# Nine bias columns instead of 37 are turned into rows, GpSimd fills its constants earlier, and the first stages stand in another order

## The reference, cut to what matters

```python
nx = layer_norm(x) ;  q = nx @ Wq ;  k = ctx @ Wk ;  v = ctx @ Wv
evidence = softmax(q k^T / sqrt(128)) @ v
combined = [nx, evidence, anchor]                      # anchor: one vector per batch
router_probs = softmax(combined @ router_W + router_b)             # 3 experts
h = silu(combined @ e_w1 + e_b1) ;  expert_out = h @ e_w2 + e_b2   # 3 x 256 hidden
g = sigmoid(silu(combined @ gate_w1 + gate_b1) @ gate_w2 + gate_b2)
x = x + g * (sum(expert_out * router_probs) @ out_w + out_b)
xq, xkv = ada_ln(x, cond), ada_ln(ctx, cond)           # silu(cond) @ Wss + bss
x = x + softmax over 16 heads of 8 (xq @ Wq + bq, xkv @ Wkv + bkv) @ Wp + bp
```

## Time and profile before

| what | value |
|---|---|
| median of 3 runs | 202.46 us (201.9 to 203.8) |
| the profiled execution | 201.29 us, its span 199.5 us |
| busy: PE, DVE, ACT, POOL | 188.9, 159.5, 126.8, 54.7 us |
| chain that ended last | PE 75%, DVE 14%, ACT 6%, issue 3% |
| HBM read, written | 11.29 MB, 2.88 MB |

### The profile page before, as it was taken

The page is one execution under the profiler, slowest core; times in us unless marked ns, Lnnn a source line. Parts: engine busy times, 40 slices in busy tenths (PEclk is TensorE's granted clock), DMA queues, the critical chain, the costliest instruction groups (busy, mean ns, idle before and its releaser), DMA issues.

```text
span 199.5 us, 4395 instructions
## 1 busy us (share of the span) xinstructions
PE 188.9 (95%) x1503; PEld 132.2 (66%) x1503; DVE 159.5 (80%) x478; ACT 126.8 (64%) x280; POOL 54.7 (27%) x75
## 2 busy tenths in 40 slices
PE   1999999999999999998999999999999999999992
PEld 0679878877767885785566856866658554566551
DVE  7747937787769999999999998999698979984021
ACT  0442458656870389578754596199929765989950
POOL 2758579949239410002470000001000200000000
PEclk9996999999999999999999999999999999999997
DMA  4991010125477000054036200032242430000001
GB/s 122 304 357 63 8 20 22 28 79 108 110 200 202 7 1 0 18 130 111 12 97 153 70 30 0 6 87 62 74 138 71 110 71 1 1 2 3 5 0 52
DMA packets 12199, 14.65 MB, mean 73 GB/s; under 512 B 1896, under 2 KB 9938, under 8 KB 11602
## 3 DMA queue, kind: packets, MB, share of 16 engines
q1 hardware_dynamic: 12120, 14.37, 26.4%
q10 hardware_dynamic: 58, 0.01, 0.0%
HBM read 11.29 MB, written 2.88 MB: 71 GB/s over the span
## 4 chain that ended last, share of the span: by engine, by line
PE 75%; DVE 14%; ACT 6%; issue 3%; POOL 0%; ACTq 0%; DVEq 0%; POOLq 0%
PE ps L735 67%; PE ps L738 8%; DVE mx L1318 5%; ACT tz L663 2%; ACT tz L672 2%; DVE hT L1241 2%; DVE xn L1177 1%; DVE bias_rows L1060 1%; DVE p L1208 1%; ACT probs L700 1%; DVE qr L1313 1%; POOL rstd L521 0%; DVE qp L1311 0%; DVE nm L1199 0%; ACT p L612 0%
## 5 line engine op out<-in xcount | busy, mean ns | idle before, releaser
L1318 DVE TENSOR_REDUCE mx<-ps 128x1 f32<-128x512 f32 x128 | 82.3, 680 | 4.1 <-PE ps L735 4.0
L700 ACT ACTIVATE probs<-ps 128x512 f32<-128x512 f32 x128 | 65.5, 603 | 6.3 <-PE ps L735 6.2
L735 PE MATMUL ps<-k_st,q_st 125*128 125x512 bf16 x128 | 38.8, 380 | 0.6 <-issue 0.6
L735 PE MATMUL ps<-q_st,k_st 128*128 128x256 bf16 x256 | 35.9, 273 | 0.2 <-DVE mx L1318 0.2
L735 PE MATMUL ps<-probs,vtile 128*32 128x256 f32 x512 | 30.9, 382 | 0.1
L735 PEld LDWEIGHTS ps<-q_st,k_st 128*128 128x128 bf16 x256 | 23.1, 98 | 11.1 <-issue 1.7
L735 PEld LDWEIGHTS ps<-probs,vtile 128*32 128x32 f32 x512 | 15.2, 109 | 12.5 <-ACT probs L700 1.8
L735 PEld LDWEIGHTS ps<-k_st,q_st 125*128 125x128 bf16 x128 | 11.8, 98 | 12.3 <-ACT probs L700 2.9
L663 ACT ACTIVATE tz<-ps,half_b 128x256 f32<-128x256 f32 x28 | 12.0, 474 | 10.0 <-PE ps L735 9.9
L1241 DVE SCALAR_TENSOR_TENSOR hT<-ps,biases,tz 128x256 f32<-128x256 f32 x28 | 12.2, 478 | 4.4 <-ACT tz L672 4.4
L529 POOL TENSOR_TENSOR rstd<-ve,mhalf 128x2 f32<-128x2 f32 x4 | 3.0, 760 | 45.0 <-DVE ve L1284 45.0
(11 more groups left out here) (173 smaller groups left out, 308.8 us busy)
## 6 DMA issues: line engine op xcount, KB each, us to landing
k_st<-k_scr SPq DMA_DIRECT2D x24, 192.0 KB
q_st<-q_scr SPq DMA_DIRECT2D x16, 144.0 KB
k_scr<-kp SPq DMA_DIRECT2D x12, 128.0 KB, 2.4
w<-in_L_xcond_e_w SPq DMA_DIRECT2D x3, 384.0 KB, 4.4
c_sb<-in_ctx SPq DMA_DIRECT2D x4, 256.0 KB, 4.5
q_scr<-qp SPq DMA_DIRECT2D x12, 64.0 KB, 2.0
x_sb<-in_x SPq DMA_DIRECT2D x4, 128.0 KB, 4.4
out<-y_sb SPq DMA_DIRECT2D x4, 128.0 KB, 2.2
```

Of the source, the lines that this page charges most:

```text
L700: A.activation(probs[:, g % 2, j, half * 2 * T:(half + 1) * 2 * T], bank("unit", b, u), ACT.Exp)\
L735: return nc.tensor.matmul(out, lhsT, rhs, start=start, stop=stop)
L1318: V.tensor_reduce(mx[:, b, t, h:h + 1], bank("tile", b, i), AX_X, ALU.max, negate=True)\
```

## The change

Four things are changed.

- The bias columns are laid out as 28 that are read as columns (seven for each batch), then the nine that are read as rows. Only the nine are split, turned (27 rows instead of 111) and sent; `bias_rows` has nine blocks instead of 37, so its memset writes 576 words in each partition instead of 2368.
- On POOL `vt0` (the constants) stands ahead of `rsx.0`; `identb` stands behind four fills of `k_st`.
- The lists are in another order: on PE `nxT.0` and `P4` stand ahead of `P2` and `P5`, `P6` stands between the two halves of `s0.0`; on ACT `nxTe.0` is the first, then `p4a`, then `ctxTe.0`. The banks of 213 of the 443 PE tokens are others. Behind batch 0 the moves are mostly of a few places.
- On SP the three stores of the first batch's keys stand in the order 2, 1, 0.

```diff
-NBZ = NZ + 1
-C_EB = B * NBZ
+C_LG = B * NZ
+C_EB = C_LG + B
 C_GB = C_EB + E
 C_BO = C_GB + 1
 NCB = C_BO + 1
+NRB = NCB - C_LG
...
     "pool": """
-        ident rsx.0 vt0 identb rsc.0 cn.0 rsx.1 zer.0 zer.1 zer.2 zer.3 zer.4 gw2h zer.5 rsx.2 rsc.2 kp.0.0 cn.2
...
+        ident vt0 rsx.0 rsc.0 cn.0 zer.0 zer.1 zer.2 zer.3 identb rsx.1 gw2h zer.4 zer.5 zer.6 zer.7 rsx.2 rsc.2
...
     "sp": """
-        ones brows k_out.0.0 k_out.0.1 k_out.0.2 k_in.0.0 k_in.0.1 k_in.0.2 k_in.0.3 q_out.0.0 k_out.1.0 q_out.0.1
...
+        ones brows k_out.0.2 k_out.0.1 k_out.0.0 k_in.0.0 k_in.0.1 k_in.0.2 k_in.0.3 q_out.0.0 k_out.1.0 q_out.0.1
...
-        half_b = sb("half_b", [P, C_EB])
+        half_b = sb("half_b", [P, C_LG])
         wide_b = sb("wide_b", [P, P])
-        bias_r = sb("bias_r", [P, 2, NCB])
-        bias_p = sb("bias_p", [P, NP, NCB], BF16)
-        bias_t = sb("bias_t", [NP * NCB, P], BF16)
-        bias_rows = sb("bias_rows", [P, NCB, P], BF16)
+        bias_r = sb("bias_r", [P, 2, NRB])
+        bias_p = sb("bias_p", [P, NP, NRB], BF16)
+        bias_t = sb("bias_t", [NP * NRB, P], BF16)
+        bias_rows = sb("bias_rows", [P, NRB, P], BF16)
...
-                mm(ot, onesb[:, 0:P], bias_rows[:, b * NBZ + NZ, 0:E], stop=False)
+                mm(ot, onesb[:, 0:P], bias_rows[:, b, 0:E], stop=False)
...
-                V.tensor_copy(bias_p[:, 0, :], biases[:]).then_inc(s["prep_dve"], 1)
+                V.tensor_copy(bias_p[:, 0, :], biases[:, C_LG:]).then_inc(s["prep_dve"], 1)
```

More of the change, by code:

```diff
@@ L48 @@
     "pe": """
[L49 to L78, removed]
@@ new lines @@
+        P1@4 ctxT.0@7 P3@6 nxT.0@4 P4@0 P2@1 P5@2 qm.0@6 P5g@4 s0.0.1@3 P6@2 s0.0.0@6 P6b P5b@7 P6c ctxT.1@6
+        p0T.0.1@1 p0T.0.0@5 P8@6 P5c@3 pc.0.0@4 nxT.1@7 pc.0.1 hkvT.0@1 qm.1@5 hid.0.0@0 hid.0.6@4 hid.0.1 P7@7
+        kproj.0@1 hid.0.2@7 hid.0.3 s0.1.1@5 hid.0.4@1 hid.0.5 lgT.0.0@2 lgT.0.1 P8b@4 vproj.0@7 s0.1.0@2 hkvT.2@3
+        eo.0.2@4 p0T.1.1@0 eo.0.3 eo.0.0@7 nxT.2@5 eo.0.1 p0T.1.0@3 ctxT.2@2 hkvT.1@1 qm.2@6 nxT.3@5 pc.1.0@3 pc.1.1
+        kproj.1@6 s0.2.0@4 lgT.1.0@7 xqT.0@5 s0.2.1@0 lgT.1.1 qproj.0@5 hid.1.2@4 hid.1.3 hid.1.4@5 hid.1.5
@@ new lines @@
+        p0T.2.1@0 hid.1.0@3 hid.1.1 vproj.1@0 kproj.2@4 qm.3@2 p0T.2.0@6 hid.1.6@5 ctxT.3@1 pc.2.0@6 tile.0.0@7
+        tile.0.1@2 tile.0.2@1 pc.2.1 tile.0.3@3 tile.0.4@5 tile.0.5@0 tile.0.6@7 tile.0.7@6 eo.1.2@4 tile.0.8@5
+        tile.0.9@7 eo.1.3 eo.1.0@3 tile.0.10@0 tile.0.11@5 tile.0.12@6 eo.1.1 tile.0.13@2 hid.2.0@1 rows.0.0@7
+        hid.2.1 tile.0.14@2 tile.0.15@0 hid.2.6@6 hid.2.2@7 hid.2.3 lgT.2.0@3 lgT.2.1 unit.0.0@5 unit.0.1@4
+        unit.0.2@1 unit.0.3@2 unit.0.4@3 hid.2.4@0 unit.0.5@7 tile.0.16@4 unit.0.6@2 hid.2.5 tile.0.17@1 s0.3.0@4
@@ new lines @@
+        tile.1.2@4 kproj.3@2 tile.1.3@7 tile.1.4@1 rows.0.3@4 tile.1.5@3 p0T.3.1@5 xqT.2@0 tile.1.6@6 tile.1.7@4
+        tile.1.8@2 tile.1.9@3 qproj.2@0 tile.1.10@7 tile.1.11@5 tile.1.12@4 pv.0.4@6 pv.0.5 unit.0.24@0 unit.0.25@3
+        pc.3.0@4 unit.0.26@6 unit.0.27@5 unit.0.28@3 pc.3.1 unit.0.29@6 tile.1.13@7 tile.1.14@1 unit.0.30@3
+        unit.0.31@5 tile.1.15@2 tile.1.16@0 tile.1.17@4 lgT.3.0@7 tile.1.18@5 tile.1.19@1 tile.1.20@6 tile.1.21@3
+        lgT.3.1 rows.1.0@0 hid.3.2@1 tile.1.22@0 hid.3.0@3 tile.1.23@6 hid.3.1 hid.3.4@2 unit.1.0@6 unit.1.1@0
@@ new lines @@
+        unit.1.2@4 unit.1.3@7 hid.3.5 tile.1.24@3 unit.1.4@7 tile.1.25@6 unit.1.5@4 unit.1.6@5 unit.1.7@0
+        tile.1.26@3 hid.3.3 tile.1.27@7 tile.1.28@0 tile.1.29@3 tile.1.30@5 tile.1.31@4 tile.2.0@6 pv.0.6@0 pv.0.7
+        tile.2.1@3 vproj.2@7 rows.1.1@0 hid.3.6@2 tile.2.2@4 oT.0.0@1 tile.2.3@7 rows.1.2@3 tile.2.4@5 oT.0.1@0
+        tile.2.5@4 tile.2.6@3 eo.3.2@2 eo.3.3 eo.3.0@5 rows.1.3@4 eo.3.1 unit.1.8@0 unit.1.9@6 unit.1.10@1
+        unit.1.11@7 unit.1.12@4 unit.1.13@2 unit.1.14@0 unit.1.15@3 tile.2.7@1 tile.2.8@5 tile.2.9@7 pv.1.0@0 pv.1.1
@@ L828, in widen_biases @@
                 pe.wait_ge(s_brows, 16)
[L829 removed]
+                mm(o[:, 0:P], onesb[:, 0:P], bias_rows[:, C_BO - C_LG, :]).then_inc(s["prep"], 1)
             def output_weights(name, part, k0, k1):
```

170 lines of the change are left out of this document (90 added, 80 removed).

## The result

The changed kernel takes **205.53 us** (204.07 to 206.31, 6 runs), the kernel before 202.38 us (201.03 to 206.1, 6 runs): a ratio of 1.0161, 95% interval [1.0118, 1.0203]. It is slower by 1.6%, some 3.2 us, and outside the forecast range of 200.3 to 204.9. The profiled execution is the slowest of the six, 206.31 us with a span of 204.5. Beside the one profiled before (201.29 us, span 199.5) it overstates the loss, so sizes in time are taken from the ratios and the mechanisms from the rows.

The account below looks back on a forecast made before the run. TensorE was taken as the bound, its start held by DMAs. P4's wait +0.7 and reordered later stages -0.1 made +0.6 us on the median 202.46: 203.1 us, range 200.3 to 204.9.

Parts of the forecast that it names:

- The bound and the early x: At the start, xn.0 ends 1.4 us earlier but gains nothing, since P5 waits for its weights until about 7.5.
- the rival: At the start, the x path was the bound: up to 1.4 us faster; no chance given.
- a fixed wall at 7.5: Ahead of P5 on TensorE, the DMA of its weights lands at about 7.5, so P5 can't start before.
- P4 ahead of P5: On TensorE before the scores, P4 waits for ACT's last small DMA until 8.5; scores start at 11.7, +0.7 us.
- With the rise at the same moment: From P5 to the scores, TensorE's pace rises at 9.6 as before, so P5 ends at 10.4 and P5g at 11.7.
- rival 3: TensorE's pace after the idle 1.6 us rises later, near 13 us: +2.4, 204.8 us; chance 0.18.
- The table load: ACT's 1.28 us load moves between nxT.0 and nxTe.0, hidden behind P5: no cost; the skill's 1380 ns drain doesn't show.
- Interleaved P6: Between 16.5 and 20 us, breaking up small products may remove the half-clock stretch: 0 or -1.7 us, taken as 0.
- rival 1: The slow stretch at 16.5 goes, since small products no longer stand together: -1.7, 201.4 us; chance 0.22.
- Smaller edits: Splits, P7, p2, fills and key stores move on no path, cost nothing; reordered later stages give -0.1 us.
- The only case in my list on this side: The slower rival, TensorE's pace rising near 13 us: 204.8 us; chance 0.18.

Follow-up runs that it names:

- The two kernels with nine columns: Changed code with the kernel before's order lists: 202.25 us, 1.0002; the same with GpSimd's constants ahead of rsx.0: 201.87 us, 0.9995.
- the two best kernels: Changed kernel with P4 back behind P5g, plus waits between three GpSimd fills (200.74 us, 0.9913) or two fills moved each way (201.83 us, 0.9952).
- the best version: Changed kernel with P4 back behind P5g and GpSimd waits ahead of fills 5, 6 and 7: 200.74 us, ratio 0.9913 to the kernel before.
- the four changed kernels without the long hold: Changed kernel with fills moved (1.0025) or gaps between fills (0.9992), and each of these with P4 behind P5g (0.9952, 0.9913).
- the first group: Changed kernel with P4 behind P5g (1.0040), fills moved (1.0025), both (0.9952); and the kernel before with P4 early (1.0022).

## Why the prediction was wrong

**The bound and the early x.** Right, within the noise. The two kernels with nine columns, 0.54 us of memset and in the second 0.60 us of cast, are at 1.0002 and 0.9995, with intervals that shut out the 1.4 us of the rival. The DMA of P5's weights is seen as P5's releaser in the two best kernels, where `nxT.0` starts at 6.34 and 6.24 and P5 at 7.70 and 7.72. It isn't a fixed wall at 7.5: with the nine columns alone P5 starts at 7.37, and with the constants moved too its releaser is `m_qk`, at 7.98.

**P4 ahead of P5.** The mechanism is right, and its first numbers too: 2.08 us of idle TensorE, P4 at 8.87, P5 at 9.69, against 1.6, 8.5 and 9.3. The size at the score was wrong: +2.8 instead of +0.7. The step that failed in it is "With the rise at the same moment": I took the pace to rise at 9.6 as before, although I had put 1.6 us of idle time just ahead of it. From P5 to the score I had 2.4 us; it took 4.12 (13.81 - 9.69). That is rival 3, to which I gave 0.18, with its sign (a pair of 128x256 at 1.06) and with its +2.4 at that place. Yet the time that it costs is 1.5 us, and 2.4 with the fills as changed: the forecast passed a delay at 11 us on to the end at full size, and that step is wrong too. In the kernel before with P4 early, 2.45 us at the score left 0.4 us.

**The table load.** Right: 6.88 to 8.16 behind `nxT.0`, `nxTe.0` at 8.17, and `qm.0` at 11.39 far behind. The function follows the load at once again, so no drain shows here either.

**Interleaved P6.** I took 0 of 0 or -1.7. In the profile after, the stretch at 16.5 is gone, with rival 1. But it is gone too in the kernel before with P4 early, where nothing is interleaved, and it is there in the profiled run of the best version, where everything is. The -1.7 was too large: the runs of the kernel before with and without the stretch are 0.4 to 0.7 us apart. Counted over runs, the new order does have it less often: a mean clock of 0.995 or more in 32 of the 48 runs of the four changed kernels without the long hold, against 11 of 101 of the kernel before. Which part of the order does that was not tried.

**Smaller edits: the step that failed most.** "`cn.0` and the fills move by 0.9, and `hkvT.0`, on TensorE at 22.17, still hides that." I asked who waits for the moved GpSimd work, and found nobody. I didn't ask whom it holds while it runs. The order table moved all four of the later fills together, behind `gw2h`, to where tile 1's cast becomes ready, and this cost 2.8 to 3.4 us, as much as the whole loss. The trace of before had a warning: the two casts of `xn.0` took 1.62 us under GpSimd's constants and 0.59 without. I used this pair of rows to shorten `xn.0` and not to price the casts that were to meet other GpSimd work. But it had the opposite too, tile 1's pair of casts in a run of five fills:

```profile
16.74 4.74 POOL L507 MEMSET k_st<- 128x1024 f32 x5
17.32 0.60 DVE L1177 TENSOR_SCALAR xn<-x_sb,mv,rstd 128x128 f32<-128x128 f32 x2
```

The first of the pair took 0.45 us. So the trace could have given a rival of up to four fills, 3.5 us, and not its chance. The order shows the four fills in a row, and the timeline of before has 0.95 us for each.

**Chances.** Undone in the order of the first group, the loss splits into -1.0 us for the rest of the change, +1.5 for P4 and +2.8 for the fills (ratios 0.9952, 1.0025, 1.0161), together +3.3. The only case in my list on this side stopped at 204.8. My range had no term for contention between two engines off TensorE.

## What to carry to other kernels

When a change moves work on an engine nobody waits for, list not only who waits for it but who shares something with it while it runs: two rows of one instruction with different durations, as 0.59 and 1.62 us here, give a price that can fall due again wherever the two come to meet. It need not: here the next meeting cost between 0.1 and 3.5 us, so it belongs among the rivals with its full size. Where long fills on GpSimd stand in a row beside casts on VectorE, a wait of GpSimd for its own last fill is cheap (0.13 us each) and took 1.7% off the changed kernel; where VectorE was not held it gave nothing. And a delay in a stage ahead of TensorE's dense part need not be worth its own length at the end (2.45 us left 0.4): undo it alone and take its price from the time.
